# Attention with score maxima by differences: a reordered work plan, two more differences a pass, and one load moved in SyncE's order

## The chip, the cores and the metric

The kernel runs on 1 core of one Trainium2 chip. The metric is the time of one execution on the device in microseconds (us); less is better. Engines are called PE (TensorE), PEld (its weight loads), DVE (VectorE), ACT (ScalarE), POOL (GpSimd) and SP (SyncE, which here issues all DMAs); SPq rows are those issues.

## The reference, cut to what matters

x is (4, 2048, 256); there are 16 heads of width 16. A feed-forward branch stands beside the attention; both are added to x.

```python
xn = layernorm(x)
q, k = rope-extended projections of xn; v = projection of xn      # (b, h, t, 16)
scores = einsum('bhqd,bhkd->bhqk', q, k) * scale                  # causal
att = softmax(where(causal, scores, -inf))
y = einsum('bhqk,bhkd->bhqd', att, v)
out = x + y @ Wc + ffn(xn)
```

## The kernel before, in words

A first part makes the weights, the projections and the feed-forward branch and stores q, k and v in DRAM; the change leaves it alone. The second part, `attention`, runs 16 passes, one for each group of 4 heads ("quad"). In this text passes are numbered 0 to 15. The 2048 queries are 4 chunks of 512.

One pass is a list of small work items, the same for PE, DVE and ACT, written out by hand in the string `TIMETABLE`. PE issues its matmuls strictly in that order; each letter is one item:

- `m`, an entry of the maxima sequence `SEQ`: a matmul of one block of 128 queries by 512 (or fewer) keys into one of 2 banks `sm`, which DVE reduces to row maxima `pm` (a plain block at L1438, a masked edge block at L1421, a paired block at L1433). Entries are also 3 transposes of the finished maxima (L1527; DVE then splits them into `mh`, `ml` and SP copies these into rows of `Q`) and 4 output projections (L1503, added by DVE at L1399). `AHEAD` entries of a pass are made already in the pass before it.
- `x`, a difference: a matmul pair with `DK` (keys 512 to 1023 minus keys 0 to 511) into one of 2 double banks `st`; ACT takes the positive part into `excess` (L1345). With it one paired block per head stands for two plain blocks, since max(a, b) = a + relu(b - a). `by_difference` says for which blocks; `NX` is the number of differences a pass.
- `s`, a score group: a matmul pair into `st`, which ACT exponentiates into `prob` (L1352). At the causal edge POOL zeroes the upper part (L1311).
- `w`, a step of the weighted sums: `pv` += `prob` x V (L1570). After the last step of each chunk ACT copies `pv` to `Y` (L1335), so there are 4 such copies a pass.

SP's DMAs of a pass stand in a fixed order in `body`, each behind a wait. In the order of the program: results of the last half pass (`move`: `scratch_l` <- Y, `Yc` <- Y), maxima rows of the third chunk (`load_m(quad, slot, 1)`), `sums`, the q and k of the quad after the next (`load_qk`, 12 DMAs), the swapped keys `KC` for the differences of the same quad (`load_kc`, 6 DMAs, L1090), V (`load_v`), then `store_inverse` and `spread_inverse` of the last half pass (SP waits between them until the stored rows have landed), `move(quad, 0)`, `load_sums(quad, 0)`, and `load_m(quad, slot, 2)` for the fourth chunk. DVE inverts what `load_sums(quad, 0)` brings (L1389) just before entry 6 of the next pass's sequence, whose items stand in this pass's list. POOL makes `DK` two quads ahead from K and KC (`difference_of_keys`, L1250 to L1264), behind the masks of the third chunk; L1253 waits for KC.

Of the kernel before, what the change touches and what calls it, by code (L numbers as in the profile page):

```python
# [22 lines left out]
NQ = B * H // G  # L23
# [742 lines left out]
GROUP_OF = {c: n for n, cs in enumerate(GROUPS) for c in cs}  # L766
LATE = 4
LEAD = 7
PROJECT_AT = (64, 77, 87, 99)
EXCESSES = 3  # L770
ROWS_LOADED = 16 * 2 * G

# [4 lines left out]

def by_difference(c, hp, t):

    return c == 3 or c == 2 and hp == 0  # L780


def maxima_sequence():
# [23 lines left out]
    for s in reversed(range(SUB)):  # L807
        sequence.insert(PROJECT_AT[s], ("project", s))
    return sequence
# [29 lines left out]
def score_units():  # L839
# [25 lines left out]


TIMETABLE = (
    "mwmxmmswxmmsmmsmwmsmsmwmmsmswsmmxwmxmmsmmmsmswsmmmswsmsmmmsmmxmxmwxm"
    "msmsmwxmmsmwsmmsmmmssmwmxmwmssmmwsmmmswsmmsmwsmmswmsmmxwsmsmmsmwsmms"
    "mwsmsmmwxmmsmwmssmmwmsmwsmsmmwmmsmswmsmsmwsmsmmwsmmsmwsmmswmsmsmwmsm"  # L870
    "mswmsmmswmsmmswmsmmswmsmxmwmsms"
)


# [68 lines left out]
def load_qk(sp, scr, quad, q, k, loaded):  # L943
    b, hq = quad // QB, quad % QB
    for name, dst, rows in (("Q", q, QROWS), ("K", k, KROWS)):
        for r, a in enumerate(rows):
            src = scr[name].rearrange("a b (q p g e) t -> a b q g e p t", p=G // 2, g=2, e=DH)[a]
            for g in range(2):
                if isinstance(quad, int):
                    one = src[b, hq, g]  # L950
                else:
                    one = src[bass.ds(b, 1), bass.ds(hq, 1), g, :, :, :].rearrange("b q e p t -> (b q e) p t")
                sp.dma_start(dst[ROW * g + r * DH:ROW * g + (r + 1) * DH, :, :], one).then_inc(loaded, 16)  # L953


def attention(nc, io, w, scr):

    with ExitStack() as ctx:
# [111 lines left out]
        def _(sp):  # L1070
            def load_v(quad):
                src = scr["V"].rearrange("n (j p) d -> n p j d", p=P)
                src = src[quad] if isinstance(quad, int) else \
                    src[bass.ds(quad, 1), :, :, :].rearrange("n p j d -> (n p) j d")
                sp.dma_start(Vr[:, :, :], src).then_inc(v_loaded, 16)
# [8 lines left out]
            def load_kc(quad):  # L1084
                b, hq = quad // QB, quad % QB
                sp.wait_ge(differed, quad) if quad else sp.wait_ge(kc_made, 1)
                for r, a in enumerate(KROWS):
                    src = scr["K"].rearrange("a b (q p g e) t -> a b q g e p t", p=G // 2, g=2, e=DH)[1 - a]
                    for g in range(2):
                        sp.dma_start(KC[ROW * g + r * DH:ROW * g + (r + 1) * DH, :, :], src[b, hq, g, :, :, 0:2 * CH]).then_inc(kc_loaded, 16)  # L1090

            def load_m(quad, slot, n, last=False):
                e = ROWS_AT[n]
                sp.wait_ge(sm_read, quad * NE + SM + 1 + (e if n < NG - 1 else NE if last else NE + e))
                cs = GROUPS[n]
                rows = SUB * len(cs)
                for r, src in enumerate((mh[n], ml[n])):
                    for g in range(2):
                        for hp in range(G // 2):
                            first = (g * (G // 2) + hp) * rows  # L1100
                            sp.dma_start(Q[slot][ROW * g + KD + r:ROW * g + KD + r + 1, hp, cs[0] * CH:(cs[-1] + 1) * CH],  # L1101
                                         src[first:first + rows, :]).then_inc(m_loaded, 16)

            def move(quad, half):
                sp.wait_ge(pv_read, quad * TC + 2 * half + 3)
                t = slice(WIDE * half, WIDE * (half + 1))
                for h in range(G):
                    row = 2 * DH * h
                    sp.dma_start(scr["L"][2 * quad + half, h:h + 1, :], Y[row + DH:row + DH + 1, t]).then_inc(y_moved, 16)
                for h in range(G):  # L1110
                    row, first = 2 * DH * h, G * DH * (quad % 2) + DH * h
                    sp.dma_start(Yc[quad // QB % 2][first:first + DH, quad % QB // 2, t], Y[row:row + DH, t]).then_inc(y_moved, 16)

            def load_sums(quad, half):
                k = 2 * quad + half
                sp.wait_ge(y_moved, 16 + MOVED * (k + 1))
                sp.dma_start(sums[:, :], L_v[k, :].rearrange("(p j) -> p j", p=P)).then_inc(sums_loaded, 16)

            def store_inverse(quad, half):
                k = 2 * quad + half  # L1120
                sp.wait_ge(inverted, k + 1)
                sp.dma_start(I_v[k, :].rearrange("(p j) -> p j", p=P), inverse[:, :]).then_inc(inverse_stored, 16)

            def spread_inverse(quad, half):
                k = 2 * quad + half
                sp.wait_ge(inverse_stored, 16 * k + 16)
                if quad >= 2:
                    sp.wait_ge(normed, 2 * (quad // 2) - 1 + half)
                for h in range(G):
                    first = G * DH * (quad % 2) + DH * h  # L1130
                    sp.dma_start(spread[half][first:first + DH, :], scr["I"][k, h:h + 1, :].to_broadcast([DH, WIDE])).then_inc(inverse_spread, 16)
# [26 lines left out]
            def load_r(g):  # L1158
                if g >= NCH - 2:
                    sp.wait_ge(pv_read, (NQ - 1) * TC + 1)  # L1160
                elif g >= 2:
                    sp.wait_ge(out_stored, 16 * (g - 1))
                sp.dma_start(residual(g), R_v[g]).then_inc(r_loaded, 16)

            def store_out(g):
                sp.wait_ge(sm_read, projected(g))
                sp.dma_start(O_v[g], residual(g)).then_inc(out_stored, 16)

            def body(quad, slot, last):
                if quad:  # L1170
                    move(quad - 1, 1)
                load_m(quad, slot, 1)
                if quad:
                    load_sums(quad - 1, 1)
                if not last:
                    if quad:
                        sp.wait_ge(pair_used, quad * STEPS)
                    nxt = (slot + 2) % SLOTS
                    load_qk(sp, scr, (quad + 2) % NQ, Q[nxt], K[nxt], qk_loaded[nxt])
                    if quad + 2 < NQ:  # L1180
                        load_kc(quad + 2)
                    sp.wait_ge(v_placed, quad + 1)
                    load_v(quad + 1)
                if quad:
                    store_inverse(quad - 1, 1)
                    spread_inverse(quad - 1, 1)
                move(quad, 0)
                load_sums(quad, 0)
                load_m(quad, slot, 2, last)
                store_inverse(quad, 0)  # L1190
                spread_inverse(quad, 0)
                if quad >= TC:
                    store_out(quad - TC)
                    for g in range(quad - TC + 2, NCH if last else quad - TC + 3):
                        load_r(g)
                if not last:
                    load_m(quad + 1, (slot + 1) % SLOTS, 0)
# [14 lines left out]
            for g in range(2):  # L1212
                load_r(g)
            quads(body)
            move_third()
            invert_third()
            for g in range(NCH - TC, NCH - 1):
                store_out(g)
            for half in range(2):
                sp.wait_ge(sm_read, projected(NCH - 1) - 1 + half)  # L1220
                t = slice(half * (SUB // 2), (half + 1) * (SUB // 2))
# [482 lines left out]
```

## Time and profile before

| | |
|---|---|
| time, median of 3 runs | 1941.61 us (1938.64 to 1945.17) |
| the profiled execution: own time, span | 1944.17 us, 1942.5 us |
| busy over the span | PE 95%, DVE 88%, ACT 81%, POOL 28% |
| granted clock of PE over the span | 0.972 of full speed |
| passes 1 to 14 | 650.5 to 1840.0 us of the span |

A pass is taken here from its first exponential (L1352) to that of the next. Its start can be read in a timeline of ACT: pass 6 begins at 1075.9, pass 7 at 1164.5, pass 14 at 1756.8 us. "Busy" of PE includes matmuls that overlap each other.

### The profile page before, as it was taken

The page shows a single profiled execution, that of the slowest core. Times are in us where ns is not written, and L with a number is a line of the kernel's source. Part 1 is how long each engine was busy: PE and PEld are TensorE (multiplying, and loading weights), DVE is VectorE, ACT ScalarE, POOL GpSimd, SP SyncE. Part 2 cuts the span into 40 slices and gives each one's busy share as a digit, 9 for nine tenths or more (in the row PEclk, how much of TensorE's full clock was granted, in tenths as well). Part 3 has the DMA queues.
Part 4 walks back from the last instruction along what each step waited for, and adds up shares of the span by engine and source line. Part 5 has one row for each costly group of instructions (what it writes and reads, how often), then busy time and mean ns, then how long its engine had stood idle before and what let it go on. Part 6 is the DMA issues. An engine that isn't in the chain of part 4 may idle for free.

```text
span 1942.5 us, 41688 instructions
## 1 busy us (share of the span) xinstructions
PE 1841.4 (95%) x13879; PEld 700.7 (36%) x13879; DVE 1712.0 (88%) x4770; ACT 1566.7 (81%) x1884; POOL 537.6 (28%) x648
## 2 busy tenths in 40 slices
PE   6899999999879999999999999999999999999998
PEld 6555565556322222222232323223232222223223
DVE  5699999999779999899998989999999899999961
ACT  2467666765349999899998989999999899999995
POOL 0122112211244131414423141432314143231211
PEclk8899999999759999999999999999999999999999
DMA  4133323334424214050522414142341514233112
GB/s 174 33 92 102 99 82 95 103 98 104 111 55 65 43 36 68 11 74 10 93 42 58 65 35 71 35 93 35 65 67 34 74 32 92 34 66 62 30 36 82
DMA packets 160324, 129.01 MB, mean 66 GB/s; under 512 B 95344, under 2 KB 144752, under 8 KB 159768
## 3 DMA queue, kind: packets, MB, share of 16 engines
q1 hardware_dynamic: 160152, 126.88, 31.1%
q8 instruction: 89, 1.46, 0.3%
q14 instruction: 83, 0.68, 0.1%
HBM read 74.60 MB, written 42.98 MB: 61 GB/s over the span
## 4 chain that ended last, share of the span: by engine, by line
PE 39%; SPq 10%; ACT 8%; DMA 7%; issue 5%; DVE 4%; POOL 1%; ACTq 0%; DVEq 0%; POOLq 0%
PE pv L1570 16%; PE st L1555 9%; PE sm L1532 9%; ACT prob L1352 6%; DMA scratch_i<-inverse 4%; SPq L1101 3%; PE sm L1503 3%; SPq L953 2%; PE st L1542 2%; ACT excess L1345 1%; SPq L1090 1%; DVE sm L1421 1%; DMA Yc<-Y 1%; DVE sm L1433 1%; DVE pm L1438 1%
## 5 line engine op out<-in xcount | busy, mean ns | idle before, releaser
L1352 ACT ACTIVATE prob<-st 128x1024 f32<-128x1024 f32 x1088 | 1058.3, 1026 | 97.1 <-PE st L1555 84.3
L1570 PE MATMUL pv<-prob,V 128*32 128x512 f32 (+3 forms) x5120 | 594.2, 546 | 4.7 <-POOL prob L1311 4.6
L1532 PE MATMUL sm<-K,Q 48*128 48x512 f16 (+3 forms) x2176 | 527.2, 352 | 28.1 <-DVE pm L1421 16.5
L1438 DVE TENSOR_REDUCE pm<-sm 128x1 f32<-128x512 f32 x768 | 493.3, 683 | 31.5 <-PE sm L1532 25.9
L1421 DVE CUSTOM_DVE_ANT_0 sm<-sm,mask 128x256 f32<-128x256 f32 (+3 forms) x1024 | 473.0, 519 | 33.2 <-PE sm L1532 31.1
L1555 PE MATMUL st<-Q,K 50*128 50x512 f16 (+3 forms) x2560 | 474.0, 354 | 22.8 <-ACT excess L1345 6.1
L1311 POOL TENSOR_SCALAR_AFFINE_SELECT prob<-prob 128x256 f32<-128x256 f32 (+1 forms) x448 | 190.3, 439 | 917.7 <-ACT prob L1352 913.9
L1532 PEld LDWEIGHTS sm<-K,Q 48*128 48x128 f16 x2176 | 160.4, 95 | 342.1 <-DVE pm L1438 143.9
L1433 DVE CUSTOM_DVE_ANT_0 sm<-sm,excess 128x512 f32<-128x512 f32 x384 | 260.0, 717 | 14.3 <-PE sm L1532 12.1
L1555 PEld LDWEIGHTS st<-Q,K 50*128 50x128 f16 x2560 | 129.4, 94 | 347.3 <-ACT prob L1352 256.2
L1345 ACT ACTIVATE excess<-st 128x1024 f32<-128x1024 f32 x188 | 189.5, 1024 | 20.0 <-PE st L1542 16.7
L1570 PEld LDWEIGHTS pv<-prob,V 128*32 128x32 f32 x5120 | 108.1, 109 | 199.7 <-issue 186.6
L1421 DVE DVE_READ_ACCUMULATOR2_ANT pm<- 128x1 f32 x1024 | 143.6, 140 | 0.0
L653 ACT ACTIVATE g<-bank 128x512 f32<-128x512 f32 x128 | 76.8, 600 | 56.1 <-PE bank L727 56.1
L688 PE MATMUL bank<-wWP,gh 128*128 128x256 f16 x512 | 113.6, 273 | 0.0
L688 PE MATMUL bank<-wWP,gl 128*128 128x256 f16 x512 | 113.5, 273 | 0.0
L538 DVE SCALAR_TENSOR_TENSOR gl<-g,wlnw,gh 128x512 f16<-128x512 f32 x128 | 92.1, 758 | 9.6 <-ACT gh L656 9.6
L473 POOL TENSOR_TENSOR frs<-fve,wmhalf 128x4 f32<-128x4 f32 x16 | 16.3, 1016 | 283.0 <-DVE fve L610 283.0
L656 ACT ACTIVATE gh<-g,wlnw 128x512 f16<-128x512 f32 x128 | 93.8, 733 | 0.0
L1542 PE MATMUL st<-DK,Q 48*128 48x512 f16 x384 | 87.7, 390 | 6.2 <-POOL DK L1264 2.5
L658 ACT ACTIVATE g<-g 128x512 f32<-128x512 f32 x128 | 81.8, 639 | 0.0
L727 PE MATMUL bank<-xh,wWF 128*128 128x512 f16 x256 | 78.1, 387 | 1.5 <-DVE xl L532 1.5
(169 smaller groups left out, 1922.7 us busy)
## 6 DMA issues: line engine op xcount, KB each, us to landing
Q<-scratch_q SPq DMA_DIRECT2D x102, 128.0 KB, 4.3
K<-scratch_k SPq DMA_DIRECT2D x102, 128.0 KB, 7.4
x<-in_x SPq DMA_DIRECT2D x16, 512.0 KB, 4.3
scratch_v<-Rt SPq DMA_DIRECT2D x64, 128.0 KB, 2.0
scratch_r<-Rt SPq DMA_DIRECT2D x16, 512.0 KB, 3.2
V_raw<-scratch_v SPq DMA_DIRECT2D x16, 512.0 KB, 9.6
Yc<-Y SPq DMA_DIRECT2D x124, 64.0 KB
spread<-scratch_i SPq DMA_DIRECT2D x124, 64.0 KB, 2.2
```

Of the source, the lines that this page charges most:

```text
L656: act.activation(gh[:, hc - 1, :], g[:, hc - 1, 0, :], ACT.Copy, scale=w["lnw"][:, hc - 1:hc])\
L688: pe.matmul(bank[s][:, 0:C], lhsT=x[:, hc, s * P:(s + 1) * P], rhs=w["WP"][:, hc, :], start=hc + k == 0, stop=hc + k == HC)
L1311: pool.affine_select(out=x, in_=x, compare_op=ALU.is_ge, fill=0.0, base=0, pattern=[[0, count], [1, P]], channel_multiplier=-1).then_inc(m ...
L1345: act.activation(excess[((slot + ahead) % SLOTS * NX + k) % EXCESSES][:, :, :], st[number % ST][:, :, :], ACT.Relu)\
L1352: act.activation(prob_of(quad, k)[:, :, :], st[number % ST][:, :, :], ACT.Exp).then_inc(exp_done, 1)
L1421: i = dve.tensor_tensor_reduce(x, x, mask[:, CH - block_width(t, k):], 1.0, -3e38, ALU.add, ALU.max, best(h, t, k))
L1433: dve.tensor_tensor_reduce(bank[:, :], bank[:, :], excess[(slot * NX + r) % EXCESSES][:, h % 2, :], 1.0, -3e38, ALU.add, ALU.max, best(h, ...
L1438: dve.tensor_reduce(out=best(h, t, k), in_=bank[:, :], axis=AX.X, op=ALU.max).then_inc(sm_read, 1)
L1532: i = pe.matmul(dst[:, at:at + width], lhsT=Q[slot][r, h // 2, t * P:(t + 1) * P], rhs=K[slot][r, h // 2, k * CH:k * CH + width], start=Tr ...
L1542: i = pe.matmul(st[number % ST][:, g, :], lhsT=Q[slot][rows[g], h // 2, t * P:(t + 1) * P], rhs=DK[slot][rows[g], h // 2, :], start=True, ...
L1555: i = pe.matmul(st[number % ST][:, a, at:at + width], lhsT=K[slot][r, hp, j * P:(j + 1) * P], rhs=Q[slot][r, hp, (c + 1) * CH - width:(c + ...
L1570: i = pe.matmul(pv[2 * DH * h:2 * DH * (h + 1), CH - width:CH], lhsT=V[quad % VSLOTS][:, j, h, :], rhs=prob_of(quad, u)[:, h % 2, at:at + ...
```

## The change

It does three things. `by_difference` now also holds for the odd query blocks of the third chunk in the second pair of heads: `NX` is 14, not 12, a pass, the sequence has 115 entries, not 119 (40 plain and 28 paired blocks where there were 48 and 24), and 6 differences are made ahead, not 4. `TIMETABLE` is written anew, with one projection entry (`PROJECT_AT`) at 75 for 77. And `load_kc` moves in SP's order from behind `load_qk` to behind `spread_inverse(quad, 0)`.

```diff
-PROJECT_AT = (64, 77, 87, 99)
+PROJECT_AT = (64, 75, 87, 99)
@@
-    return c == 3 or c == 2 and hp == 0
+    return c == 3 or c == 2 and (hp == 0 or t % 2 == 1)
@@ TIMETABLE = (
-    "mwmxmmswxmmsmmsmwmsmsmwmmsmswsmmxwmxmmsmmmsmswsmmmswsmsmmmsmmxmxmwxm"
...
+    "wsmmswxmmwmsmsmmsmmswmmsmxwxmmsmwmxmsmmsmmsmwsmmsmwsmmsmwmxmxmmsmmxw"
...
@@ in body of sync
                     load_qk(sp, scr, (quad + 2) % NQ, Q[nxt], K[nxt], qk_loaded[nxt])
-                    if quad + 2 < NQ:
-                        load_kc(quad + 2)
                     sp.wait_ge(v_placed, quad + 1)
                     load_v(quad + 1)
@@
                 store_inverse(quad, 0)
                 spread_inverse(quad, 0)
+                if quad + 2 < NQ:
+                    load_kc(quad + 2)
                 if quad >= TC:
```

The stretch of the list from the last `w` of the second chunk to entry 6 (at whose place DVE inverts the sums), both ends included, is

```python
before = "wmssmmwsmmmswsmmsmwsmmswmsmmxwsmsmmsm"
after  = "wmsmsmwmmsmswsmmmswxmmswsmmsmwsmm"
```

SP's order in one pass, before, from the loads of q and k on (`Q<-mh`, `Q<-ml` with 1x4x128 are the maxima rows of one chunk):

```order
L953 DMA Q<-scratch_q 16x2x2048 x6
L953 DMA K<-scratch_k 16x2x2048 x6
L1090 DMA KC<-scratch_k 16x2x1024 x6
L1075 DMA V_raw<-scratch_v 128x16x64
L1122 DMA scratch_i<-inverse 128x32
L1131 DMA spread<-scratch_i 16x1024 x4
L1109 DMA scratch_l<-Y 1x1024 x4
L1112 DMA Yc<-Y 16x1024 x4
L1117 DMA sums<-scratch_l 128x32
L1101 DMA Q<-mh 1x4x128 x4
L1101 DMA Q<-ml 1x4x128 x4
```

The same with the change, from V to the rows of the next pass's first chunks:

```order
L1075 DMA V_raw<-scratch_v 128x16x64
L1122 DMA scratch_i<-inverse 128x32
L1131 DMA spread<-scratch_i 16x1024 x4
L1109 DMA scratch_l<-Y 1x1024 x4
L1112 DMA Yc<-Y 16x1024 x4
L1117 DMA sums<-scratch_l 128x32
L1101 DMA Q<-mh 1x4x128 x4
L1101 DMA Q<-ml 1x4x128 x4
L1122 DMA scratch_i<-inverse 128x32
L1131 DMA spread<-scratch_i 16x1024 x4
L1090 DMA KC<-scratch_k 16x2x1024 x6
L1101 DMA Q<-mh 1x8x128 x4
```

The 6 KC loads have moved from ahead of V to behind the second `spread`; the sums and the fourth chunk's rows are among what they now stand behind.

DVE's order before, in the last query block of the third chunk and its edge blocks (L1433 with its read of the accumulator is a paired block, L1438 a plain one):

```order
L1433 ISA sm,pm<-sm,excess 128x512
L1433 ISA pm 128x1
L1433 ISA sm,pm<-sm,excess 128x512
L1433 ISA pm 128x1
L1396 COPY idle<-sm 128x1
L1438 TENSOR_REDUCE pm<-sm 128x1 x4
L1421 ISA sm,pm<-sm,mask 128x512
L1421 ISA pm 128x1
```

The same place with the change:

```order
L1433 ISA sm,pm<-sm,excess 128x512
L1433 ISA pm 128x1
L1433 ISA sm,pm<-sm,excess 128x512
L1433 ISA pm 128x1
L1433 ISA sm,pm<-sm,excess 128x512
L1433 ISA pm 128x1
L1433 ISA sm,pm<-sm,excess 128x512
L1433 ISA pm 128x1
L1396 COPY idle<-sm 128x1
L1421 ISA sm,pm<-sm,mask 128x512
L1421 ISA pm 128x1
```

Four plain blocks have become two paired ones, here and at one more place of the pass.

PE's order before, around the transpose (L1527) of the fourth chunk's maxima:

```order
L1542 MATMUL st<-DK,Q 128x512 x2
L1570 MATMUL pv<-prob,V 32x512 x4
L1555 MATMUL st<-Q,K 128x512 x2
L1532 MATMUL sm<-K,Q 128x128
L1532 MATMUL sm<-K,Q 128x384
L1555 MATMUL st<-Q,K 128x512 x2
L1527 MATMUL sm<-ident,m 128x128
L1532 MATMUL sm<-K,Q 128x128
L1532 MATMUL sm<-K,Q 128x384
L1555 MATMUL st<-Q,K 128x512 x2
```

The same with the change:

```order
L1542 MATMUL st<-DK,Q 128x512 x2
L1532 MATMUL sm<-K,Q 128x256 x4
L1555 MATMUL st<-Q,K 128x512 x2
L1570 MATMUL pv<-prob,V 32x512 x4
L1555 MATMUL st<-Q,K 128x512 x2
L1532 MATMUL sm<-K,Q 128x128
L1532 MATMUL sm<-K,Q 128x384
L1532 MATMUL sm<-K,Q 128x128
L1532 MATMUL sm<-K,Q 128x384
L1555 MATMUL st<-Q,K 128x512 x2
L1527 MATMUL sm<-ident,m 128x128
L1570 MATMUL pv<-prob,V 32x512 x4
```

The difference stands further ahead of the transpose, and the two edge entries stand together before it.

## Rows read from the trace of the kernel before

**Rows 1.** The page: busy time; the exponentials (busy, mean ns, idle before)

```profile
PE 1841.4 (95%) x13879; PEld 700.7 (36%) x13879; DVE 1712.0 (88%) x4770; ACT 1566.7 (81%) x1884; POOL 537.6 (28%) x648
...
L1352 ACT ACTIVATE prob<-st 128x1024 f32<-128x1024 f32 x1088 | 1058.3, 1026 | 97.1 <-PE st L1555 84.3
```

**Rows 2.** Windows, one for each of passes 1 to 14

```profile
core 0: us, PE busy (x) PEld busy (x) DVE busy (x) ACT busy (x) POOL busy (x), PEclk, DMA share, GB/s
650.50:734.90 84.40, 80.85 (x659) 23.48 (x655) 78.14 (x242) 78.89 (x86) 28.01 (x36) 0.98 0.27 45
...
1075.90:1164.50 88.60, 84.41 (x667) 25.00 (x659) 79.14 (x241) 78.73 (x85) 27.96 (x36) 0.96 0.32 55
...
1756.80:1840.00 83.20, 81.59 (x667) 24.57 (x659) 79.11 (x241) 78.74 (x85) 15.22 (x30) 1.00 0.29 54
sum 1189.50, PE 1147.46 PEld 342.36 DVE 1105.49 ACT 1102.71 POOL 379.25; mean PE 81.96 PEld 24.45 DVE 78.96 ACT 78.77 POOL 27.09
```

**Rows 3.** Timelines of DVE and PE, pass 6: start, length, [idle before <- releaser]

```profile
1123.24 0.35 DVE L1389 RECIPROCAL inverse<-sums 128x32 f32<-128x32 f32 x1 [2.75 <-DMA sums<-scratch_l]
```

```profile
1124.41 0.60 PE L1532 MATMUL sm<-K,Q 48*128 48x512 f16 x1 [2.84 <-DVE pm L1421]
...
1128.62 1.93 PE L1570 MATMUL pv<-prob,V 128*32 128x512 f32 x8
...
1131.64 1.07 PE L1570 MATMUL pv<-prob,V 128*32 128x512 f32 x8
```

**Rows 4.** Timeline of DVE in pass 14

```profile
1801.26 0.34 DVE L1389 RECIPROCAL inverse<-sums 128x32 f32<-128x32 f32 x1
```

**Rows 5.** Timeline of SP's DMA issues in pass 6

```profile
1098.75 2.75 SPq L1090 DMA_DIRECT2D KC<-scratch_k  x6
...
1102.01 7.63 SPq L1122 DMA_DIRECT2D scratch_i<-inverse  x1
1114.12 1.72 SPq L1131 DMA_DIRECT2D spread<-scratch_i  x4
1115.88 1.15 SPq L1109 DMA_DIRECT2D scratch_l<-Y  x4
...
1121.64 0.37 SPq L1117 DMA_DIRECT2D sums<-scratch_l  x1
```

**Rows 6.** The same in pass 14, which loads no KC

```profile
1780.16 6.13 SPq L1122 DMA_DIRECT2D scratch_i<-inverse  x1
1789.04 2.87 SPq L1131 DMA_DIRECT2D spread<-scratch_i  x4
...
1797.31 0.35 SPq L1117 DMA_DIRECT2D sums<-scratch_l  x1
...
1807.19 2.42 SPq L1131 DMA_DIRECT2D spread<-scratch_i  x4
```

**Rows 7.** Timelines of DVE and ACT where blocks follow each other closely

```profile
1280.00 0.73 DVE L1433 CUSTOM_DVE_ANT_0 sm<-sm,excess 128x512 f32<-128x512 f32 x1
...
1280.65 1.28 DVE L1438 TENSOR_REDUCE pm<-sm 128x1 f32<-128x512 f32 x2
```

```profile
1076.90 1.02 ACT L1345 ACTIVATE excess<-st 128x1024 f32<-128x1024 f32 x1
1077.82 1.02 ACT L1352 ACTIVATE prob<-st 128x1024 f32<-128x1024 f32 x1
```

**Rows 8.** Timeline of POOL in pass 8 (1247.8 to 1332.2 us)

```profile
1299.11 2.37 POOL L1270 TENSOR_TENSOR Yc<-Yc,spread 128x1024 f32<-128x1024 f32 x1
...
1304.50 2.13 POOL L1253 TENSOR_TENSOR apart<-KC 128x1024 f32<-128x1024 f16 x1
...
1313.20 2.37 POOL L1264 TENSOR_TENSOR DK<-apart 128x1024 f16<-128x1024 f32 x1
1326.01 0.41 POOL L1311 TENSOR_SCALAR_AFFINE_SELECT prob<-prob 128x256 f32<-128x256 f32 x1 [10.45 <-ACT prob L1352]
```

**Rows 9.** All DMA issues by line, us to landing last

```profile
KC<-scratch_k SPq DMA_DIRECT2D x96, 64.0 KB, 8.3
```

More of the change, by code:

```diff
@@ L867 @@
 TIMETABLE = (
-    "mwmxmmswxmmsmmsmwmsmsmwmmsmswsmmxwmxmmsmmmsmswsmmmswsmsmmmsmmxmxmwxm"
-    "msmsmwxmmsmwsmmsmmmssmwmxmwmssmmwsmmmswsmmsmwsmmswmsmmxwsmsmmsmwsmms"
-    "mwsmsmmwxmmsmwmssmmwmsmwsmsmmwmmsmswmsmsmwsmsmmwsmmsmwsmmswmsmsmwmsm"
-    "mswmsmmswmsmmswmsmmswmsmxmwmsms"
+    "wsmmswxmmwmsmsmmsmmswmmsmxwxmmsmwmxmsmmsmmsmwsmmsmwsmmsmwmxmxmmsmmxw"
+    "msmsmwsmmmxmswsmmsmsmmsmwmsmsmwmmsmswsmmmswxmmswsmmsmwsmmsmwsmsmmxwm"
+    "smmswmsmmswsmmmswxmwmssmmwsmsmmmswsmmswsmmmswsmmswsmmmswsmmswsmsmmms"
+    "wxmmmswsmmswmsmmxwmsmmswxmmms"
 )
```

## The prediction, made before the changed kernel ran

> **What bounds the kernel now.** I read the page first. Over the span PE is busy 1841.4 us, DVE 1712.0 and ACT 1566.7, and exponentials wait 97.1 us in all, mostly for PE's score matmuls [rows 1]. These are averages over two parts; so the next view is the windows, cut at the first exponential of each pass [rows 2]. Three things are to be seen there. DVE (79.1 us) and ACT (78.8) do the same in every pass and are nearly level, so neither alone is the bound: PE issues one ordered list for both, each with two banks, and each waits a little in turn. Second, the best passes take 83.2 us. Third, other passes do the same work and take up to 88.6 us: passes 1 to 14 take 1189.5 us where 14 of the best would take 14 x 83.2 = 1164.8. The 24.7 us between are stalls, and the granted clock is below 1.00 in the worst of those passes.
>
> The worst is pass 6. There DVE stands 2.75 us at the reciprocal, for the load of `sums` [rows 3]. DVE is in order: the edge blocks behind it keep the `sm` banks full, PE cannot fill its next entry (2.84 us idle) [rows 3], and ACT is fed by the same list. The reciprocal starts 1123.24 - 1075.9 = 47.3 us into this pass; in pass 14, of 83.2 us, it starts 44.5 us in, with no wait [rows 2, 4]. 2.9 us late cost 88.6 - 83.2 = 5.4 us, since PE afterwards ran at its lower level, 1.2 GHz: the same eight matmuls of a weighted sum take 1.93 us right behind the stall and 1.07 us three microseconds later [rows 3].
>
> A page of the Trainium skill bears on this: "TensorE: Matmul & The Clock Gate", on HAM oscillation, holds that every stretch at the lower clock costs half its length. The windows of passes 1 to 14 give a clock of 0.98 four times and 0.96 twice, which is some 28 us at 1.2 GHz, so by the page 14 of the 24.7 us would be clock and the rest the waits themselves. The trace agrees in pass 6 roughly: 6.8 us at 1.2 GHz makes 3.4, and 2.84 of idle makes 6.2, against 5.4 measured.
>
> Why are the sums late? In pass 6 SP issues KC at 1098.75, then V, then the store of the inverse at 1102.01; that issue alone takes 7.63 us and its landing releases SP only at 1114.12, so `scratch_l` goes out at 1115.88 and the sums' load at 1121.64, 45.7 us into the pass [rows 5]. Pass 14 loads no KC: `spread` starts 32.2 us in, where pass 6 has 38.2, and the sums' load is issued 40.5 us in [rows 6]. So the queue ahead of the store, KC among it, is what makes SP late.
>
> **The change, part by part.** *KC behind the urgent transfers.* Removed from ahead of the store are 2.75 us of issue and 6 x 64 KB [rows 5, 9]. What that is worth I take from pass 14: the sums go out at 40.5 instead of 45.7 us in the worst pass, and land 1123.24 - 1121.64 = 1.6 us later at most, at 42.1 [rows 3, 5, 6].
>
> "DMA: Bandwidth & Descriptors" of the Trainium skill, on HWDGE ordering, says that each DMA engine consumes its descriptors in ring order; by that the store lies behind all of KC's bytes, which fits. It gives no sum of its own here.
>
> *The reciprocal is due earlier.* In the quoted stretch of the list from the second chunk's last `w` to entry 6 there are 13 `s` and `x` before and 11 after, 17 `m` before and 15 after. ACT adds 0.92 us for each instruction that follows closely [rows 7], so the place comes 2 x 0.92 = 1.8 us earlier, at 42.7 us. Sums at 42.1 still make it, by 0.6 us; and what precedes SP's loads is also shorter (the third chunk's transpose stands behind 11 instead of 12 `s` and `x`, one copy fewer), which is worth about a microsecond more of slack. I take: no stall here, in 14 passes. Saved: 24.7 us.
>
> *Fourth chunk's rows.* Its transpose and its first score group are 7 instead of 6 `s` and `x` apart: 0.9 us more room. I count nothing.
>
> *The differences.* Per pass 8 plain blocks go and 4 paired ones come. A plain block takes 1.28 us for two, the second adding about 0.60; a paired one 0.65 from start to start [rows 7]. DVE: -8 x 0.60 + 4 x 0.65 = -2.2 us. ACT: +2 x 0.92 = +1.8 us [rows 7]. PE loses 4 half-array matmuls and gains 2 pairs, nothing. So 79.1 and 78.8 become 76.9 and 80.6 by the windows' measure. Bounds: if the pass follows the mean of the two, it falls by 0.2, and to 82.2 (an estimate) if the new order also saves a quarter of the 4.1 us that DVE idles in a pass of 83.2; if ACT's idle time there, 83.2 - 78.8 = 4.4 us, stays whole, the pass takes 85.0. ACT waits for PE, which is held up by DVE's banks too, and DVE has less to do; so I take neither gain nor loss: 83.2 us.
>
> *KC arrives later.* Pass 14 ends its first-half `spread` 1807.19 + 2.42 - 1756.8 = 52.8 us in [rows 6]; 1.8 us earlier makes 51.0, six KC issues end at 53.8, and with the median landing of 8.3 us [rows 9] KC is there by 62 us; POOL's L1253, at 56.7 us in pass 8, then starts 5.3 us late, and `DK` is done 11.1 us behind it, at 73, or 75.5 with a normalisation of 2.4 ahead of the masks. The first mask of the fourth chunk is due at 78.2 us [rows 8]. Hidden by at least 2.7 us; the next user of `DK` is a pass away. The next rows behind KC in SP's order are those of the next pass's first chunks, whose transpose stands late in the list. Zero.
>
> *First and last pass.* Both stay: in the last one the list has as many differences as before; the first is long through the handover from the first part, at a low clock. The two more differences ahead of pass 0 fall into ACT's idle time there. Zero.
>
> **Sum.** 1944.17 (own time of the profiled execution) - 24.7 = 1919.5 us. The median of the runs is 2.6 us below that execution: 1917.
>
> **Rivals.** (A) *The reciprocal comes earlier but its sums do not.* If q and k alone fill the queue, the sums stay where they are and the place moves 1.8 us ahead. Against it: pass 14. For it: pass 14's store still took from 1780.16 to 1789.04 to release SP, and 0.6 us is thin. Price: between 1.0 and 1.9 us (5.4 / 2.9) for each microsecond late, so 1.8 to 3.4 us a pass, 25 to 47 us over 14: 1967 to 1989. It breaks even where the sums come 1.8 us earlier than now. Chance 0.11 for the kernel being slower by this, from 1948 up.
>
> (B) *ACT becomes the bound.* Stalls go, but its 1.8 us are paid in full: 14 x 85.0 = 1190.0, against 1189.5 now: 1942, no change. For it: ACT's idle gaps, 97.1 us in all, are waits for PE that each `w` in the list brings [rows 1], and a difference is another item in the same queue. Against it: DVE falls by more. Chance 0.11.
>
> (C) *Stalls only halved,* because other late transfers remain: 1929, within the range. It shares the forecast's sign; chance 0.13, with 0.65 for the forecast itself.
>
> **How the numbers follow.** Likeliest is 1917. Packing at 82.2 us a pass, 15 passes, would take 15 off: 1902, and a shorter pass 0 a few more, so the low end is 1900. Upward the range takes in (C) and (B): 1943; above lies (A), 0.11, and below the low end some 0.05. A run of this kernel can tell about 0.3%, 6 us, from no change. Faster: 0.65 + 0.13 - 0.01 = 0.77; same, (B) with a bit of (A)'s edge: 0.11; slower: 0.12.
>
> **What would show it.** Right: passes of equal length near 83 us; `spread` near 32 us and the sums' load at 40 us or earlier in every pass; no DVE wait for `sums`; clock 1.00 in the windows of passes 1 to 14; DVE near 76.9 and ACT near 80.6 us a pass. Wrong: reciprocals that wait in most passes (A); all passes at 85 us and ACT without gaps (B); POOL's L1253 waiting for KC beyond 62 us, with weighted sums of the fourth chunk waiting for masks.

## The result, and the profile after

The changed kernel takes 1915.51 us (median of 4 runs, 1912.73 to 1919.89) against 1943.39 for the kernel before: a ratio of 0.9864, 95% interval 0.9835 to 0.9892. The forecast was 1917. The profiled execution spans 1910.9 us, where before it was 1942.5: 31.6 less. Its page, with the busy times and the exponentials' row (compare [rows 1]):

```profile
span 1910.9 us, 41847 instructions
...
PE 1832.3 (96%) x13879; PEld 695.6 (36%) x13879; DVE 1678.8 (88%) x4770; ACT 1582.8 (83%) x1916; POOL 538.3 (28%) x648
...
L1352 ACT ACTIVATE prob<-st 128x1024 f32<-128x1024 f32 x1088 | 1047.7, 1029 | 62.7 <-PE st L1555 53.5
```

The windows of passes 1 to 14, cut as in [rows 2] (length, busy times, clock, DMA):

```profile
647.80:731.60 83.80, 80.63 (x653) 23.02 (x651) 75.96 (x240) 79.53 (x86) 28.07 (x36) 0.98 0.25 45
731.60:817.00 85.40, 82.20 (x654) 23.03 (x653) 76.13 (x240) 79.61 (x87) 28.07 (x36) 0.96 0.28 44
817.00:899.00 82.00, 79.00 (x653) 22.82 (x651) 75.91 (x240) 79.47 (x87) 28.07 (x36) 1.00 0.28 46
...
1063.90:1146.40 82.50, 81.52 (x662) 24.41 (x659) 77.14 (x240) 79.80 (x88) 28.07 (x36) 1.00 0.29 59
...
sum 1159.60, PE 1138.72 PEld 337.12 DVE 1076.45 ACT 1115.85 POOL 379.90; mean PE 81.34 PEld 24.08 DVE 76.89 ACT 79.70 POOL 27.14
```

From pass 3 on every pass takes 82.0 to 83.0 us at clock 1.00. Passes 1 to 14 give back 1189.5 - 1159.6 = 29.9 us; the part up to pass 1 gives 650.5 - 647.8 = 2.7, and the last pass with the end takes 103.5 instead of 102.5. That is the 31.6.

The chain that stalled DVE, in pass 6 of the changed kernel: SP's issues, then DVE's reciprocal (compare [rows 3], [rows 5]):

```profile
1087.22 0.91 SPq L1075 DMA_DIRECT2D V_raw<-scratch_v  x1
1088.18 5.32 SPq L1122 DMA_DIRECT2D scratch_i<-inverse  x1
1096.08 1.72 SPq L1131 DMA_DIRECT2D spread<-scratch_i  x4
1097.84 1.15 SPq L1109 DMA_DIRECT2D scratch_l<-Y  x4
...
1103.32 0.36 SPq L1117 DMA_DIRECT2D sums<-scratch_l  x1
...
1116.58 3.00 SPq L1090 DMA_DIRECT2D KC<-scratch_k  x6
```

```profile
1107.85 0.35 DVE L1389 RECIPROCAL inverse<-sums 128x32 f32<-128x32 f32 x1
```

`spread` starts 32.2 us into the pass (38.2 before), the sums' load goes out at 39.4 (45.7), and the reciprocal at 43.9 us waits for nothing. Over passes 4 to 14 `spread` starts 33.4 us in on the mean (35.8 before) and the sums' load goes out at 40.9 (43.4), at the latest at 42.2. No early reciprocal waits in any pass.

`sm` has three banks (`SM` is 3 in the code), where the text and the prediction ahead of this have two. No number of the forecast rests on it.

### The profile page after: what moved, and what is told of

It is laid out like the page before. It is cut to its first block, busy times and chain, and to the rows that moved or that the text cites. A ratio compares the mean times of both kernels' runs of the same rounds, so it can differ in the third digit from the quotient of the medians.

```text
span 1910.9 us, 41847 instructions
## 1 busy us (share of the span) xinstructions
PE 1832.3 (96%) x13879; PEld 695.6 (36%) x13879; DVE 1678.8 (88%) x4770; ACT 1582.8 (83%) x1916; POOL 538.3 (28%) x648
## 4 chain that ended last, share of the span: by engine, by line
PE 45%; ACT 14%; issue 7%; DVE 5%; POOL 1%; SPq 1%; DMA 0%; DVEq 0%; ACTq 0%; POOLq 0%
PE pv L1570 18%; ACT prob L1352 12%; PE st L1555 10%; PE sm L1532 10%; PE sm L1503 4%; PE st L1542 2%; DVE sm L1433 2%; ACT excess L1345 1%; DVE sm L1421 1%; DVE pm L1438 1%; DVE pm L1421 0%; DVE pm L1433 0%; PE sm L1527 0%; ACT Y L1335 0%; POOL apart L1262 0%
## 5 line engine op out<-in xcount | busy, mean ns | idle before, releaser
L1352 ACT ACTIVATE prob<-st 128x1024 f32<-128x1024 f32 x1088 | 1047.7, 1029 | 62.7 <-PE st L1555 53.5
L1532 PE MATMUL sm<-K,Q 48*128 48x512 f16 (+3 forms) x2112 | 479.8, 350 | 16.5 <-DVE pm L1421 6.9
L1438 DVE TENSOR_REDUCE pm<-sm 128x1 f32<-128x512 f32 x640 | 412.6, 684 | 40.3 <-PE sm L1532 37.0
L1433 DVE CUSTOM_DVE_ANT_0 sm<-sm,excess 128x512 f32<-128x512 f32 x448 | 301.3, 711 | 16.8 <-PE sm L1532 16.0
L1532 PEld LDWEIGHTS sm<-K,Q 48*128 48x128 f16 x2112 | 151.4, 95 | 325.6 <-DVE pm L1433 109.2
L1555 PEld LDWEIGHTS st<-Q,K 50*128 50x128 f16 x2560 | 125.2, 94 | 370.3 <-ACT prob L1352 270.4
L1345 ACT ACTIVATE excess<-st 128x1024 f32<-128x1024 f32 x218 | 220.6, 1025 | 9.1 <-DVE pm L1438 4.7
L1542 PE MATMUL st<-DK,Q 48*128 48x512 f16 x448 | 98.6, 391 | 3.6 <-POOL DK L1264 2.4
L473 POOL TENSOR_TENSOR frs<-fve,wmhalf 128x4 f32<-128x4 f32 x16 | 16.3, 1016 | 283.0 <-DVE fve L610 283.0
```

The lines of the kernel that those rows point to most:

```text
L1345: act.activation(excess[((slot + ahead) % SLOTS * NX + k) % EXCESSES][:, :, :], st[number % ST][:, :, :], ACT.Relu)\
L1352: act.activation(prob_of(quad, k)[:, :, :], st[number % ST][:, :, :], ACT.Exp).then_inc(exp_done, 1)
L1433: dve.tensor_tensor_reduce(bank[:, :], bank[:, :], excess[(slot * NX + r) % EXCESSES][:, h % 2, :], 1.0, -3e38, ALU.add, ALU.max, best(h, ...
L1438: dve.tensor_reduce(out=best(h, t, k), in_=bank[:, :], axis=AX.X, op=ALU.max).then_inc(sm_read, 1)
L1532: i = pe.matmul(dst[:, at:at + width], lhsT=Q[slot][r, h // 2, t * P:(t + 1) * P], rhs=K[slot][r, h // 2, k * CH:k * CH + width], start=Tr ...
L1542: i = pe.matmul(st[number % ST][:, g, :], lhsT=Q[slot][rows[g], h // 2, t * P:(t + 1) * P], rhs=DK[slot][rows[g], h // 2, :], start=True, ...
```

## The experiments

Twelve kernels, each timed beside the kernel before. The ratios are to that kernel.

**1. Only KC moved** (`kc_move_only`): the old list, the old differences.

```diff
                     load_qk(...)
-                    if quad + 2 < NQ:
-                        load_kc(quad + 2)
...
                 spread_inverse(quad, 0)
+                if quad + 2 < NQ:
+                    load_kc(quad + 2)
```

> The kernel before, with nothing changed but the place of the KC loads, which go behind the second spread. Theory 1 (KC ahead of the store of the inverse makes SP late, the sums miss the reciprocal, and that is the 24.7 us that passes 1 to 14 took over 14 x 83.2): about 1919 us against 1943; every pass from 1 to 14 near 83.2 us, the sums' load issued 39 to 41.5 us into the pass, no wait of VectorE for it. Theory 2 (the gain came from the new order and the differences, and KC only moved along): 1935 us or more.

Measured: 1927.29 us, ratio 0.9932 (0.9906 to 0.9958), which is 13 us. The windows of passes 1 to 14 together, and of pass 7:

```profile
653.40:1822.80 1169.40, 1137.73 (x9210) 338.44 (x9206) 1104.66 (x3349) 1102.72 (x1177) 379.86 (x498) 1.00 0.30 55
1154.20:1237.40 83.20, 81.55 (x667) 24.42 (x659) 79.07 (x241) 78.72 (x85) 28.05 (x36) 1.00 0.30 58
```

20.1 of the 24.7 us are gone and the best pass is still 83.2 us, so theory 1 holds for the place. In the old list the move is worth 13 us, about half of the change's 26 (ratio 0.9864). (The profiled execution lost 4.3 us again outside these passes.) Of the 4.6 us that stay over 14 x 83.2, pass 2 has 1.3, with a stretch at 1.2 GHz, and passes 9 and 12 (84.2 and 84.7 us) have 2.5. No early reciprocal waits any more, but in those two passes PE waits 1.2 and 1.3 us for the fourth chunk's rows (`Q<-ml`). In passes 1 to 14 together PE waits for them (total, times, longest):

```profile
PE st L1555 <- DMA Q<-ml: 5.5, 12, 1.3
```

In the kernel before it is 2.0 us, where DVE's stall comes first; in the changed kernel there is no such wait.

**2. KC back in the changed kernel** (`kc_move_undone`), the reverse edit.

> The changed kernel with the KC loads back in their old place, behind q and k. Theory 1: the sums are as late as before while the new list wants them 1.8 us earlier, so the reciprocal waits in nearly every pass, 1.8 us more than before, at 1.0 to 1.9 us for each microsecond: 1960 to 1990 us, slower than the kernel before. Theory 2: 1925 us or less.

Measured: 1935.35 us, ratio 0.9977 (0.9949 to 1.0005). Neither theory: the kernel is not the 20 to 50 us slower than the one before that theory 1 gave. In the traces passes 1 to 14 take 1175.9 us, 16.3 more than with the change; by the timed runs (0.9977 against 0.9864, from two comparisons) moving KC is worth 22 us in the new list, where it was 13 in the old, and the list and the differences without the move 4.5 us, with an interval that includes no change at all. 13 and 4.5 don't make 26: the two parts may help each other, but each interval is 5 us or more to either side, so this isn't shown.

The longest wait of the reciprocal, in pass 11:

```profile
1536.97 0.35 DVE L1389 RECIPROCAL inverse<-sums 128x32 f32<-128x32 f32 x1 [3.20 <-DMA sums<-scratch_l]
```

In passes 4 to 14 the reciprocals run 1.2 us later than 43.9 on the mean, as they ran 1.2 us later than 44.5 before. Its place came forward by 0.6 us only, not by 1.8: the copy of the second chunk starts later in the new list (32.5 us into the pass, 31.8 before), and from there to the reciprocal it is 11.4 us instead of 12.7. These 1.3 us are about what DVE's two fewer entries are worth (0.60 each [rows 7]), not ACT's 1.8.

**3. The reciprocal later, KC unmoved** (`recip_later`), in the kernel before.

```diff
-INVERT_EARLY, INVERT_LATE = LATE + 2, PROJECTS[2] + 1
+INVERT_EARLY, INVERT_LATE = LATE + 10, PROJECTS[2] + 1
```

> The kernel before, KC in its old place, with the early reciprocal taken 8 entries later in VectorE's order (behind entry 13 instead of 5). Theory 1 (the stall is VectorE waiting for the sums): the sums still arrive late but nobody waits for them; what is left is the fourth chunk's rows, whose copies SP issues late in the same passes. About as fast as with KC moved: 1925 to 1932 us against 1942. Rival (the wait for the sums is only a sign, the late rows of the fourth chunk cost the same): 1940 us.

Measured: 1934.91 us, ratio 0.9965 (0.994 to 0.9991): 7 us. In its pass 10 (1402.9 to 1489.2, 86.3 us) the sums are late, nobody waits for them, and the next user of the late SP does. Waits from 1448 to 1463 us:

```profile
ACT prob L1352 <- PE st L1555: 3.9, 3, 2.1
...
PEld st L1555 <- DMA Q<-ml: 2.3, 1, 2.3
...
PE st L1555 <- DMA Q<-ml: 1.8, 1, 1.8
```

So by the timed runs the sums explain about half of what moving KC brings (7 of 13 us, with intervals that overlap), and the fourth chunk's rows, behind them in SP's order, have a part in the rest. Over passes 1 to 14 of this trace PE waits for them more than in kernel 1 (5.5 us):

```profile
PE st L1555 <- DMA Q<-ml: 9.2, 13, 2.4
```

**4. KC in its old place, a sixteenth of its bytes** (`kc_small`), in the kernel before.

```diff
-sp.dma_start(KC[..., :, :], src[b, hq, g, :, :, 0:2 * CH])
+sp.dma_start(KC[..., :, 0:64], src[b, hq, g, :, :, 0:64])
```

> The kernel before, KC in its old place and with its 6 issues, but each moves 64 of 1024 columns (a sixteenth of the bytes; the rest of KC is left out, so the differences are wrong). Theory 1a (bytes ahead of the store make it late): as with KC moved, 1927 us, spread at 32 to 35 us into the pass. Theory 1b (SP's 2.8 us of issuing make it late): still 1940 us, spread at 35 to 38 us.

Measured: 1927.38 us, ratio 0.9913 (0.9884 to 0.9942), as good as moving KC. SP in its pass 6 (1071.0 us on):

```profile
1093.85 2.75 SPq L1090 DMA_DIRECT2D KC<-scratch_k  x6
...
1097.12 3.66 SPq L1122 DMA_DIRECT2D scratch_i<-inverse  x1
1104.90 1.81 SPq L1131 DMA_DIRECT2D spread<-scratch_i  x4
```

The issues take their 2.75 us as before, yet `spread` starts 33.9 us into the pass, not 38.2. By its time this is 1a: taking the bytes out of the queue is enough. SP's rows are less clear. Over passes 4 to 14 `spread` starts 34.6 us in on the mean, where the kernel before has 35.8 and kernel 1 has 33.0: the bytes give 1.2 of the 2.8 us by which SP comes earlier, and the rest may be the 2.75 us of issuing. The reverse test, all the bytes with less issuing ahead of the store, was not made.

**5. The old list with 14 differences** (`old_order_14`): KC moved, four `m` fewer and two `x` more, placed by hand.

```diff
-PROJECT_AT = (64, 77, 87, 99)
+PROJECT_AT = (62, 73, 83, 95)
-LEAD = 7
+LEAD = 8
-AHEAD = 58
+AHEAD = 56
-    "mwmxmmswxmmsmmsmwmsmsmwmmsmswsmmxwmx...
+    "mwmxmmswmmsmmsmwssmxwmmsmswsmmxwmxmm...
```

(`by_difference` as in the change.)

> The old list with KC moved and the two more differences put in by hand: four plain blocks fewer a pass, two difference items more, the difference items next to them shifted a little so that their three buffers come free in time, everything else where it was. Against the kernel with only KC moved: if neither engine is the bound alone, within 5 us of it. If ScalarE is the bound by now, 1.8 us a pass more, 27 us in all. If VectorE is, up to 2.2 us a pass less, 30 us.

Measured: 1992.89 us, ratio 1.0266 (1.0233 to 1.03). Passes 1 to 14 take 1233.2 us, 88 each; even those at clock 1.00 take 86.8 to 87.7. This doesn't price the two differences, only my placing of them. Waits in the first 25 us of its pass 8:

```profile
DVE sm L1421 <- PE sm L1532: 4.7, 4, 2.0
...
ACT prob L1352 <- PE st L1555: 3.0, 4, 1.6
```

Where four blocks went out, DVE starves. PE stands before a difference meanwhile, 1.10 us at 1280.76 us, until ACT's exponential frees an `st` bank.

**6. The new list with 12 differences** (`new_order_12`): the two `x` out, the four `m` back beside their partners; `PROJECT_AT` (68, 79, 91, 103), `AHEAD` 60, `by_difference` as before.

> The changed kernel with 12 differences a pass again: the two difference items are taken out of its list and the four plain blocks put back at their places. It tells whether the new order's 82.4 us a pass need the differences. If neither engine is the bound alone, 83 to 84 us a pass, 1918 to 1930 us. If VectorE is the bound, its 2.2 us come back in full: 84.6 us a pass, 1945 us. If the differences only cost, 1910 us or less.

Measured: 1941.18 us, ratio 1.0001 (0.9978 to 1.0024). Undisturbed passes take 84.1 us. Waits of ACT for score groups in its pass 11, then in the changed kernel's pass 11, then in pass 7 of `kc_move_only`:

```profile
ACT prob L1352 <- PE st L1555: 4.8, 11, 0.9
```

```profile
ACT prob L1352 <- PE st L1555: 1.7, 6, 0.5
```

```profile
ACT prob L1352 <- PE st L1555: 2.7, 9, 0.7
```

The new list is made for 14: with the four blocks back at their two places it is worse than the old one by 0.9 us a pass.

**7 and 8. Less work for one engine.** `dve_less` is kernel 1 with the four blocks reduced over 32 columns; `act_less` is the changed kernel with the two added positive parts over 16.

```diff
+part = bank[:, 0:32] if t in (9, 11) and h >= 2 and k == 1 else bank[:, :]
-dve.tensor_reduce(out=best(h, t, k), in_=bank[:, :], ...)
+dve.tensor_reduce(out=best(h, t, k), in_=part, ...)
```

```diff
+n = 16 if k in (2, 5) else CH
-act.activation(excess[...][:, :, :], st[number % ST][:, :, :], ACT.Relu)
+act.activation(excess[...][:, :, 0:n], st[number % ST][:, :, 0:n], ACT.Relu)
```

> The old list with only KC moved, and the four plain blocks a pass that the two more differences would remove reduced over 32 columns instead of 512, so some 2 us a pass are left out of VectorE's work and nothing is added to ScalarE's. If VectorE's work is what the old list waits for: up to 2 us a pass less, 1900 us. If the two engines wait for each other in turn: about half, 1912 us. If it is hidden: 1927 us.

Measured: 1929.23 us, ratio 0.9922 (0.9891 to 0.9952); kernel 1 has 0.9932. The window of passes 1 to 14:

```profile
653.80:1825.10 1171.30, 1139.12 (x9210) 338.12 (x9206) 1079.53 (x3349) 1102.78 (x1178) 380.76 (x498) 1.00 0.31 55
```

DVE does 25 us less than in kernel 1, and the passes take as long. Hidden: in the old list, what these four blocks cost DVE is no part of the 83.2 us.

> The changed kernel with the positive parts of the two added differences a pass taken over 16 instead of 512 columns of each bank (the paired blocks then add zeros), so some 1.6 us a pass are left out of ScalarE's work. If ScalarE is the bound after the change: 1.6 us a pass less, 25 us, 1890 us. If its added work lies in its idle time: 1915 us.

Measured: 1909.61 us, ratio 0.9832 (0.9799 to 0.9865). ACT does 19 us less; passes 4 to 14 take 907.8 us against 908.4. So there ACT's added work at these two places costs next to nothing. The rest of the gain is in passes 1 to 3 (245.9 us against 251.2), where this execution kept its clock:

```profile
649.40:895.30 245.90, 236.91 (x1957) 68.37 (x1953) 227.50 (x718) 234.40 (x258) 84.34 (x109) 1.00 0.29 46
```

This may not be chance: the mean granted clock of its five runs is 0.974 to 0.977, that of the changed kernel's four 0.972 or 0.973. Whether ACT's added work costs some 5 us by way of the clock is open; the two intervals of the ratio overlap.

**9. Full matmuls in passes 0 to 3** (`busy_projects`), in the changed kernel.

```diff
-pe.matmul(dst[:, 0:1], lhsT=w["ident"][:, :], rhs=w["ident"][:, 0:1], ...)
+for a in range(2 * CC):
+    i = pe.matmul(dst[:, a * P:(a + 1) * P], lhsT=w["ident"][:, :], rhs=w["ident"][:, :], ...)
```

> The changed kernel with TensorE given the work of the output projections in passes 0 to 3 too, where there is nothing to project yet and the list holds a matmul of one column in their place: four of 128 columns. If the thin stretch of these passes is why the clock falls to 1.2 GHz in passes 1 and 2 (83.8 and 85.4 us against 82.0 in pass 3), both fall to 82.4 and the whole to 1911 us. If the added matmuls only cost: 1918 us or more.

Measured: 1912.72 us, ratio 0.9843 (0.9812 to 0.9874). Its windows of passes 1, 2 and 3:

```profile
645.90:728.80 82.90, 81.58 (x678) 25.52 (x677) 76.36 (x240) 80.00 (x88) 28.07 (x36) 1.00 0.28 46
728.80:811.60 82.80, 81.50 (x678) 25.40 (x677) 76.23 (x240) 79.91 (x87) 28.02 (x36) 1.00 0.27 46
811.60:894.10 82.50, 81.33 (x677) 25.48 (x675) 76.20 (x240) 79.89 (x87) 28.05 (x36) 1.00 0.28 46
```

TensorE does more, and the three passes take 248.2 us instead of 251.2, at clock 1.00; its six runs have a mean clock of 0.975 to 0.978. Pass 3, which kept its clock before too, takes 82.5 us for 82.0. But the thin stretch isn't shown to be the whole cause: kernel 8 kept the clock with the one-column matmuls in place.

**10 to 12. Going on from the change.** `after_recip_later` takes the reciprocal at `LATE + 6`; `v_later` moves `load_v` behind `load_sums(quad, 0)`; `all_three` has both and edit 9.

```diff
                     load_qk(...)
-                    sp.wait_ge(v_placed, quad + 1)
-                    load_v(quad + 1)
...
                 load_sums(quad, 0)
+                if not last:
+                    sp.wait_ge(v_placed, quad + 1)
+                    load_v(quad + 1)
                 load_m(quad, slot, 2, last)
```

> The changed kernel with the early reciprocal 4 entries later. In its trace the sums' load was issued up to 42.2 us into a pass and the reciprocal ran at 43.9 without a wait. If sums are sometimes late in other executions, this takes a few us and some of the spread away: 1912 us. If they are always in time: 1915 us, no difference.

> The changed kernel with the load of V (512 KB) also taken from ahead of the store of the inverse, to behind the sums' load. Spread at 28 to 31 us into the pass instead of 31 to 35, the sums' load at 38.4 in every pass. If the changed kernel has no stall from this chain left, no gain: 1915 us. If V then delays the fourth chunk's rows: slower by 1 us a pass, 1930 us.

> The later reciprocal, the full matmuls in passes 0 to 3 and V behind the sums, together in the changed kernel. If the first two gain what they may and V costs nothing: 1908 us. If nothing is left to gain from the chain: as the one with the matmuls alone.

Measured: 1912.63 us, 0.985 (0.9818 to 0.9882); 1914.11 us, 0.9844 (0.9814 to 0.9874); 1911.13 us, 0.983 (0.9801 to 0.986; 1908.37 to 1912.24). SP in pass 7 of `v_later` (1150.1 us on):

```profile
1172.82 0.35 SPq L1122 DMA_DIRECT2D scratch_i<-inverse  x1
1181.32 1.72 SPq L1131 DMA_DIRECT2D spread<-scratch_i  x4
1188.60 0.35 SPq L1117 DMA_DIRECT2D sums<-scratch_l  x1
```

The sums go out at 38.5 us and the pass is still 82.6 us; passes 4 to 14 take 908.3 us against 908.4: that chain has nothing left to give. (Passes 1 to 3 take 255.8 us in this trace, all at clock 0.96.) All four intervals (kernels 9 to 12) overlap that of the changed kernel. `all_three` has the lowest median of these three, and each of its runs lies below each of the changed kernel's (1912.73 at the least), but these were measured in different comparisons; it may be 2 to 4 us better, which isn't shown.

## Why the prediction was right

*The time* was right to 1.5 us, and part of that is luck. In the profiled executions 31.4 us went (1944.17 to 1912.73 us), where the sum had 24.7. It was hit because the forecast took the profiled execution to lie 2.6 us above its median, and the one of the changed kernel lies 2.8 below its own. The direction was right, and so was the cause of the stalls; the sizes of the terms were off.

*"Saved: 24.7 us", the stalls.* Right in its mechanism: most of it was SP's lateness, taking KC's bytes out of the queue is enough against it (kernel 4), and moving KC ends DVE's waits (kernels 1 and 2). Too large for the move alone: 20.1 us in the old list's trace, 16.3 in the new, 13 and 22 by the timed runs. Passes 1 and 3 of the kernel before, 84.4 us each, have a stretch at 1.2 GHz and no wait for the sums; I had counted them as stalls of the same kind, and passes 1 and 2 of the changed kernel still have such stretches.

*The fourth chunk's rows: "I count nothing."* This was a term. With KC moved and the old list, PE waits for these rows in 12 of 14 passes, 5.5 us in all (kernel 1). With the new list it never does, and not even with KC in its old place (kernel 2). The "0.9 us more room" would explain it. How much of the new list's gain this is was not tested by itself.

*"So I take neither gain nor loss: 83.2 us."* This failed in its size. The undisturbed pass went to 82.4 us: 14 x 0.8 = 11.2 us, near the lower bound of 82.2. The differences' effect on both engines was forecast well (DVE 76.9 forecast and measured, ACT 80.6 against 79.7), but neither is where the time comes from: 25 us less of DVE changed nothing in the old list (kernel 7), 19 us less of ACT nothing in passes 4 to 14 of the new (kernel 8). The order gives it, together with the differences it was made for: exponentials wait 62.7 us for their scores instead of 97.1, and kernels 5 and 6 show that either list with the other's number of differences loses 0.9 to 5 us a pass against the old list. Which of its many local moves does it is open.

*"The place comes 2 x 0.92 = 1.8 us earlier, at 42.7 us."* A wrong step that did no harm, by luck. The place is at 43.9 us; I counted ACT's instructions, and the two fewer entries of DVE fit better (kernel 2). The sums came later than forecast too: 42.1 us was to be the worst, and in the trace they land 40.1 to 43.9 us into the pass, in nine of the 14 passes later than 42.7. In pass 4 they are there within 0.1 us of the reciprocal. The sign "the sums' load at 40 us or earlier in every pass" was missed (38.4 to 42.2), and so was clock 1.00 in passes 1 and 2. The two misses, of the place and of the sums, offset each other. Rival A fell all the same: even with KC in its old place the kernel isn't slower than before.

*KC arrives later.* Right and cheaper. In pass 6 POOL:

```profile
1121.39 2.13 POOL L1253 TENSOR_TENSOR apart<-KC 128x1024 f32<-128x1024 f16 x1 [1.25 <-DMA KC<-scratch_k]
...
1130.09 2.38 POOL L1264 TENSOR_TENSOR DK<-apart 128x1024 f16<-128x1024 f32 x1
...
1140.35 0.41 POOL L1311 TENSOR_SCALAR_AFFINE_SELECT prob<-prob 128x256 f32<-128x256 f32 x1 [7.88 <-ACT prob L1352]
```

KC is there at 57.5 us, `DK` is done at 68.6 and the mask due at 76.4. The row of KC's issues shows why, beside [rows 9]: behind the four `spread` loads instead of q and k, 64 KB land in 2.2 us, not 8.3.

```profile
KC<-scratch_k SPq DMA_DIRECT2D x96, 64.0 KB, 2.2
```

*Rival B* fell: 1159.6 / 14 = 82.8 us a pass, not 85.0. *Rival C*, stalls half removed, is what the timed runs show for the move in the old list (13 of 24.7 us); the new list made up for it.

## What to carry to other kernels

A load that nobody needs soon is not free ahead of urgent ones in a queue: its price is read from the landing of the small store behind it, and where that store releases the issuing engine, everything it issues afterwards moves with it. Find every waiter behind the late engine, not the first alone: removing the first wait shows the second (PE's wait for the rows grew from 2.0 to 5.5 us when DVE's for the sums went). And when two engines share one ordered list, their totals don't say what a change of mix is worth; test it by taking the work away at that place.

## What the runs showed of the hardware that was not expected

TensorE's clock fell to 1.2 GHz without an idle stretch of TensorE. In pass 2 of the changed kernel, where the list has a one-column matmul for a projection (L1496), from 735.21 us on (start, length, [idle before]):

```profile
735.21 0.38 PE L1496 MATMUL sm<-ident 128*128 128x1 f32 x2
735.86 0.39 PE L1532 MATMUL sm<-K,Q 48*128 48x512 f16 x1 [0.27 <-DVE pm L1433]
...
736.86 0.39 PE L1555 MATMUL st<-Q,K 50*128 50x512 f16 x2
737.18 1.92 PE L1570 MATMUL pv<-prob,V 128*32 128x512 f32 x8
...
740.79 1.07 PE L1570 MATMUL pv<-prob,V 128*32 128x384 f32 x16
```

The eight matmuls of a weighted sum take 1.92 us here and 1.07 at full clock [rows 3] (the last row, with the clock back, has 16 shorter ones); the longest idle time of PE in the ten microseconds before is 0.27 us. Full matmuls in those places kept the clock at 1.00 in all three passes (kernel 9). So did less work for ACT, with the one-column matmuls left in (kernel 8), so what the fall needs is open.

The issue of one 16 KB store took SP 5.32 us behind the queued loads (4.1 to 8.8 us in passes 1 to 14 of the changed kernel) and 0.35 us where V was no longer ahead of it. Yet the store has not landed that much earlier: from the start of its issue to that of `spread`, which waits for the landing, it is 10.3 us with V ahead and 8.1 without, on the mean of passes 4 to 14.
